# Two-layer GNN kernel: a second rounded copy of layer 0's split rows in two PSUM banks, the product halves in one bank, the last sums of a pair turned behind the next pair's first chunks

## What is computed

```python
agg = jax.ops.segment_sum(x[src], dst, num_segments=N)          # both layers
h = (1.0 + eps) * x + agg                                       # layer 0
h = relu(batch_norm(h @ W1 + b1, g1, be1)); h = relu(batch_norm(h @ W2 + b2, g2, be2))
x = layernorm(x + (x + h))
h = jnp.where(indeg[:, None] > 0, agg, x)                       # layer 1, indeg: edges of a node
h = batch_norm(relu(h @ W.T + b)); x = layernorm(x + h)
```

## Time and profile before

| | us |
|---|---|
| median of 3 runs | 2592.99 (2587.13 to 2593.28) |
| the profiled execution | 2588.04, its span 2586.3 |
| PE busy | 2295.0 (89% of the span) |
| POOL busy | 1602.0 (62%) |
| DVE busy | 1364.4 (53%) |
| ACT busy | 801.0 (31%) |
| granted TensorE clock, mean | 0.950 |

### The profile page before, as it was taken

How to read it: one execution, slowest core, us unless ns; L and a number is a source line. 1 busy time by engine, 2 the same in 40 slices (tenths; PEclk the granted TensorE clock), 3 DMA queues, 4 the chain that set the end, 5 groups by cost and what they waited for, 6 DMA issues and landing times. The chain is left out here.

```text
span 2586.3 us, 41697 instructions
## 1 busy us (share of the span) xinstructions
PE 2295.0 (89%) x9657; PEld 1505.0 (58%) x9658; DVE 1364.4 (53%) x2155; ACT 801.0 (31%) x1272; POOL 1602.0 (62%) x1729
## 2 busy tenths in 40 slices
PE   4999999999999999799995299999999999999964
PEld 2666666666666666688884255555555555555544
DVE  5555555555555555533336555455545555554557
ACT  1333333333333333455548411111111111111157
POOL 6777777777777777100002467777777777777712
PEclk9999999999999999899996699999999999999976
DMA  8777778787877877433216767777777777777758
GB/s 259 233 227 242 224 236 245 220 249 231 242 242 225 251 222 245 142 112 95 93 49 190 255 193 223 210 225 220 219 224 213 226 222 217 223 225 216 224 138 285
DMA packets 180571, 545.11 MB, mean 211 GB/s; under 512 B 48787, under 2 KB 51178, under 8 KB 175794
## 3 DMA queue, kind: packets, MB, share of 16 engines
q0 software_dynamic: 125120, 410.09, 53.5%
q1 hardware_dynamic: 33880, 78.23, 10.1%
q10 hardware_dynamic: 21544, 56.48, 6.5%
HBM read 493.06 MB, written 51.62 MB: 211 GB/s over the span
## 5 line engine op out<-in xcount | busy, mean ns | idle before, releaser
L780 PE MATMUL psum<-ring,select 128*125 x2600 | 1260.9, 608 | 11.0 <-issue 8.7
L555 POOL DMA_INDIRECT ring<-x_in,staged x782 | 799.1, 1022 | 246.2 <-issue 224.0
L555 POOL DMA_INDIRECT ring<-x_d,staged x782 | 748.2, 957 | 261.4 <-issue 226.4
L780 PEld LDWEIGHTS psum<-ring,select 128*125 128x125 f32 x2600 | 479.3, 191 | 380.3 <-issue 336.0
L651 DVE TENSOR_TENSOR rows_lo<-ring,rows_hi 128x512 fp32r<-128x512 f32 x500 | 329.8, 689 | 283.8 <-ACT rows_hi L867 283.2
L867 ACT ACTIVATE rows_hi<-ring 128x512 fp32r x500 | 295.0, 625 | 479.3 <-SPq L523 335.9
L808 PE MATMUL psum<-sumsT_hi,w_hi 128*128 128x250 f32 x1248 | 400.6, 321 | 4.3 <-DVE sumsT_lo L674 4.3
L765 PE MATMUL psum<-rows_hi,select_r 128*125 128x512 f32 x500 | 376.0, 752 | 7.5 <-DVE rows_lo L651 4.2
L808 PE MATMUL psum<-sumsT_lo,w_hi 128*128 128x250 f32 x1248 | 350.1, 281 | 0.0
L808 PE MATMUL psum<-sumsT_hi,w_lo 128*128 128x250 f32 x1248 | 348.4, 279 | 0.0
L808 PEld LDWEIGHTS psum<-sumsT_hi,w_hi 128*128 128x128 f32 x1248 | 237.3, 190 | 36.1 <-issue 32.6
(11 more groups left out here) (168 smaller groups left out, 2255.2 us busy)
## 6 DMA issues: line engine op xcount, KB each, us to landing
hidden_d<-of_layer ACTq DMA_DIRECT2D x25, 1000.0 KB, 5.4
act_f<-hidden_d SPq DMA_DIRECT2D x24, 1000.0 KB
ring<-x_in,staged POOLq DMA_INDIRECT x782, 3.8
ring<-x_d,staged POOLq DMA_INDIRECT x782, 3.7
own<-x_in ACTq DMA_DIRECT2D x50, 224.0 KB
own<-x_d ACTq DMA_DIRECT2D x50, 224.0 KB
ring<-x_d SPq DMA_DIRECT2D x10, 1120.0 KB
x_d<-done_r SPq DMA_DIRECT2D x9, 1120.0 KB
```

The source lines that it names most:

```text
L555: nc.gpsimd.indirect_dma_start(slot(s), None, table, bass.IndirectOffsetOnAxis(ap=staged[:, s:s + 1], axis=0)).then_inc(gathered[s], 16)
L780: whole = nc.tensor.matmul(agg(h), select[h][:, WHOLE_AT.index(p), :], of_chunk(pe, first, place), start=False, stop=n + 1 == WINDOW, skip ...
```

## The change

1. Layer 0: ACT writes each high part twice, to `rows_hi` for PE and to PSUM bank 5 or 7 for DVE, which subtracts from there. So ACT waits, before the pair of writes of k, for DVE to be done with k - 2.
2. Layer 0: bank 5 is freed by putting all products of the loop in bank 4 (one bank in place of two). The very last ones use banks 4 and 0.
3. Both layers: PE clears bank 0, starts the pair's first two chunks, and only then waits for the second tile's sums, clears bank 1 and turns (`between` in `scatter`).
4. Layer 1: the edge counts are taken out of `selection` and stand later in DVE's order (`counts`).

```diff
+        high_ps = [m.bank(5), m.bank(7)]
+        AHEAD = 2 if layer == 0 else 0
+        PRODUCT_BANKS = 1 if layer == 0 else 2
+        def prod_ps(b, last):
+            return m.bank(4 if b % 2 == 0 or layer == 0 and not last else 0 if layer == 0 else 5)
...
@@ low_rows
-                        nc.vector.tensor_tensor(rows_lo[:, k, :], of_chunk(dve, first, SPLIT_AT[k]),
-                                                rows_hi[:, k, :].bitcast(F32), ALU.subtract).then_inc(split_lo, 1)
+                        high = high_ps[k % 2] if layer == 0 else rows_hi[:, k, :].bitcast(F32)
+                        nc.vector.tensor_tensor(rows_lo[:, k, :], of_chunk(dve, first, SPLIT_AT[k]), high, ALU.subtract
+                                                ).then_inc(split_lo, 1)
@@ DVE's loop
                         low_part(v)
+                        if layer == 1:
+                            counts(v, 0)
...
                         low_rows(v, 1, first[1], 0, 4)
+                        if layer == 1:
+                            counts(v, 1)
@@ scatter
                     for n, p in enumerate(ORDER):
+                        if n == 2:
+                            between()
@@ turn
                     for h in range(2):
                         pe.wait_ge(sums_done[h], job + 1)
+                    if bank is not None:
+                        at = within(pe, bank * m.BANK, 2 * m.BANK, "bank 1 or 2")
+                        clear(m.psum[0:z.NT, bass.ds(at, 1)])
@@ PE's loop
-                    clear(i, 0)
-                    clear(i, 1)
+                    pe.wait_ge(sums_done[0], i * groups + 1)
+                    clear(agg(0)[:, 0:1])
+                    pe.reg_mov(cleared, 1)
                     with pe.Fori(0, groups) as g:
                         v = of_use(pe, i, groups, g)
-                        turn(v)
-                        scatter(i, v, g, tiles(i, 0), 0)
-                        scatter(i, v, g, tiles(i, 1), 1)
+                        scatter(i, v, g, tiles(i, 0), 0, lambda: turn(v, pe.snap(cleared, min_val=1, max_val=2)))
+                        scatter(i, v, g, tiles(i, 1), 1, lambda: None)
+                        pe.reg_mov(cleared, 2)
@@ high_rows
                         act.wait_ge(split_used, SPLIT * (2 * v + h) + k + 1)
+                        if layer == 0:
+                            act.wait_ge(split_lo, SPLIT * (2 * v + h) + k + 1)
                         act.wait_ge(landed, i * per_pair + first + (SPLIT_AT[k] + 1))
-                        nc.scalar.activation(rows_hi[:, k, :], of_chunk(act, first, SPLIT_AT[k]), ACT.Copy
-                                             ).then_inc(split_hi, 1)
+                        high = nc.scalar.activation(rows_hi[:, k, :], of_chunk(act, first, SPLIT_AT[k]), ACT.Copy)
+                        if layer == 0:
+                            high = nc.scalar.activation(high_ps[k % 2].bitcast(F32R), of_chunk(act, first, SPLIT_AT[k]),
+                                                        ACT.Copy)
+                        high.then_inc(split_hi, 1)
```

More of the change, by code:

```diff
@@ L602, in _ @@
                 if layer == 0:
+                    nc.vector.sem_inc(split_lo, AHEAD)
+                if layer == 0:
                     setup.vector(dve)
@@ L638, in selection, with counts @@
                                             ).then_inc(select_done[h], 1)
[L639 to L646, removed]
+                def counts(v, h):
+                    dve.wait_ge(select_done[h], 2 * v + 2)
+                    with nc.allow_low_precision(reason="counts up to WINDOW are exact in bfloat16"):
+                        nc.vector.tensor_reduce(edge_count[h][:, 0, :],
+                                                select_r[h][:].bitcast(F32).rearrange("p k n -> p n k"), AX.X, ALU.add)
+                        nc.vector.tensor_reduce(edge_count[h][:, 1, :], select[h][:].rearrange("p k n -> p n k"),
+                                                AX.X, ALU.add).then_inc(counted[h], 1)
                 def low_rows(v, h, first, a, b):
@@ L747, in agg, with clear, scatter @@
                     return m.bank(h)[0:z.NT, :]
[L749 to L754, removed]
+                def clear(out):
+                    nc.tensor.matmul(out, m.zeros[:, 0:z.NT], m.ones[:, 0:1], start=True, stop=False,
+                                     skip_group_check=True)
+                def scatter(i, v, g, tile, h, between):
                     tile_use = pe.snap(2 * v + h)
@@ L785, in scatter, with turn @@
                             product(v, PRODUCT_AT[h][n + 1])
-                def turn(job):
+                def turn(job, bank=None):
                     pe.wait_ge(lo_done, 2 * job + 1)
@@ L796, in turn, with product @@
                     last.then_inc(turned, 1)
-                def product(job, b):
+                def product(job, b, final=False):
                     if b == 0:
@@ L801, in product @@
                         pe.wait_ge(weights_lo, W_PARTS)
-                    pe.wait_ge(product_out, HALVES * job + b + 1)
+                    pe.wait_ge(product_out, HALVES * job + b + (1 if layer == 1 or b == 0 or not final else 0))
                     for o in (2 * b, 2 * b + 1):
-                        out = prod_ps[:, b % 2, (o % 2) * z.W:(o % 2 + 1) * z.W]
+                        out = prod_ps(b, final)[:, (o % 2) * z.W:(o % 2 + 1) * z.W]
                         parts = [(w, s, k) for k in range(z.KD)
@@ L832, in _ @@
                 for b in range(HALVES):
-                    product(uses, b)
+                    product(uses, b, final=True)
             @block.scalar
             def _(act):
-                nc.scalar.sem_inc(product_out, 2)
+                nc.scalar.sem_inc(product_out, PRODUCT_BANKS)
                 if layer == 0:
@@ L875, in read_product @@
                     for o in (2 * b, 2 * b + 1):
-                        from_ = prod_ps[:, b % 2, (o % 2) * z.W:(o % 2 + 1) * z.W]
+                        from_ = prod_ps(b, last)[:, (o % 2) * z.W:(o % 2 + 1) * z.W]
                         if layer == 0:
@@ L884, in read_product @@
                     nc.scalar.sem_inc(product_out, 1)
-                    if layer == 0 and b == HALVES - 1 and store:
+                    if layer == 0 and b == HALVES - 1 and not last:
                         act.dma_start(m.hidden_d[bass.ds(pair * P, P), :], hidden.rearrange("p k n -> p (k n)")
@@ L929, in _ @@
                 for b in range(HALVES):
-                    read_product(uses, z.PAIRS - 1, b, store=False)
+                    read_product(uses, z.PAIRS - 1, b, last=True)
 def batch_norm_constants(nc, z, m, dve_sem, act_sem, dve, act, gamma, beta, scale, bias, blocks, tmp):
```

9 lines of the change are left out of this document (6 added, 3 removed).

## The result

| | before | after |
|---|---|---|
| median, us | 2593.14 (2587.13 to 2593.32, 4 runs) | 2562.97 (2558.62 to 2565.32, 4 runs) |
| the profiled execution | 2588.04 | 2563.73, its span 2562.0 |
| mean granted TensorE clock | 0.950 | 0.964 |

The forecast was 12.5 us.

What follows compares the result with a forecast made beforehand. Two limits within 3%, PE's sequence and POOL's gathers, were taken to bound both layers; afterwards PE sets layer 0. Layer 0 -1.5 and layer 1 -11 us made 2593 - 12.5 = 2580.5 us, range 2545 to 2606.

Steps and rivals of the forecast that it cites:

- the second copy at 0.50: Layer 0, ACT: each extra write of a high part to PSUM was taken to cost 0.50 us, bounds 0 to 0.53.
- k0: Layer 0, first split row of a pair's first tile: PE ready at 3.0, row at 4.4, stall 1.4 us.
- k6: Layer 0, split row behind product 0: ready 3.8 us after the product's end, PE wants it at 3.5, 0.3 late.
- From the first of these activations to k2 pass 2.64 us.: Layer 0, ACT: split row k2 starts 2.64 us after the turned sums' first activation, stalling PE 1.75 us.
- E + 10.6: Layer 0, E being PE's end of a pair's last chunk: product 0 starts 10.6 us after it, 1.05 us late.
- rival 1: Layer 0 becomes bound by the gathers, if k0 and k2 come 1.2 us sooner: 2524 to 2551 us; 15%.
- the start point was 40.40: Layer 0 before: mean 40.40 us a pair against PE's own 38.97, the 1.4 us lost to the gathers.
- Rival 2: Layer 0 split rows' chain costs more than the turn gives, PE's idle spots risk a low clock: 2611 us; 20%.
- Forecast -11: Layer 1 in all: earlier start, faster gathers and shorter end give -11 us, between -4 and -16.
- The 3 us from the gathers: Layer 1: gathers at 1.25 us set the time after POOL's restart; up to 7 us less, 3 taken.
- the 2 us at the end: Layer 1: last turn follows the last gather after 10.7 us, in layer 0 after 8.8; 2 us gained.
- The single product bank: Product loop: ACT needs 1.4 us to read a product, 4 us lie between products; no cost unless ACT is 3 us late.

## Why the prediction was right in sign and short in size

**Right: what bounds layer 0.** Gathers beside `low_rows` are lengthened by its two SBUF operands, and the read from PSUM takes all of the excess away (1.024 to 0.948 us). The Trainium skill ("SBUF — State Buffer", Who interferes with whom) states the contention, and the traces agree in both layers (layer 1: 0.966 to 0.945). What it says of a probe, in which `tensor_tensor` didn't stall DMAs, doesn't carry over to these gathers: with nothing changed but the place of that operand they take 1.004 and 0.948 us. That PE would then set the pace, POOL waiting for it, was right as well (20.3 us), and so was the second copy at 0.50 (0.58 busy, a distance of 0.52 to 0.54).

**Right: k0, and k6 nearly.** k0's wait was 1.25 us (forecast 1.4), k6 costs 0.1 (0.3).

**The step that failed: "From the first of these activations to k2 pass 2.64 us."** It stacked k2 behind the second copy. But that stretch is not set by ACT's own row of work: it begins when PE has turned, and the own-row loads are issued while the activations still run (the load of 249.45 stands ahead of the activation of 249.95). The extra copies fit in between, k2 starts 3.9 us after the turn's start in both kernels, and the 2.64 us are 1.93 (249.95 to 251.88). Product 0 comes at E + 9.7 in the pair shown instead of the forecast E + 10.6. Over the 23 pairs of the changed kernel from one E to the next the median is E + 9.82; over the 10 pairs of the kernel before that ran at full clock and took at most 39.3 us it was E + 9.45. The term was 1.05 us a pair and is 0.4. Those 10 pairs took 39.06 us at the median; with k6's 0.1 that gives 39.55, and 39.53 was measured, where the forecast had 40.3. 24 x 0.77 = 18.5 us, less 1 us more in the first pair (it lost 2.0 instead of 1): layer 0 gained 19.1 us instead of 1.5. The prediction weighed "k2 1.2 us sooner" as rival 1; k2 came 0.8 us sooner, and the result lies between the forecast and that rival. That the sum came within 18 us of the median is in part luck: layer 0 was forecast 17.6 us too slow and layer 1 8.4 us too fast.

**What was missing: why the start point was 40.40.** The prediction put it to the gathers alone and used the low clock only as a risk. The runs show two limits of equal pace: with the gathers freed and the turn early, low clocks hold a pair at 40.87 us; with the turn late and the gathers not freed (and no copy), the gathers hold it at 40.37; freed gathers and a full clock together give 39.53, or 39.60 with the early turn filled. Rival 2 had it that new idle spots of PE would lower the clock. Between the second and the last turn of layer 0 there was no low clock left at all. The waits for k0 and k2 stand apart, between matmuls, and the wait and the turn no longer stand in one piece; that this is the reason is argued, not shown.

**Layer 1: the sign right, the size too large.** Forecast -11, and -2.6 in the profile. The start was nearly right: the 21st gather came 4 us sooner (32.7 to 28.8; forecast 5 to 6). With the early turn it came as soon (28.8), so that this is the late counts' doing. The 3 us from the gathers did not come, and of the 2 us at the end 0.7. The mean gather went from 0.957 to 0.966 us: as many as before overlap a subtraction, which here still reads two SBUF operands (91 and 90), but 34 instead of 21 take longer than 1.1 us. With the early turn, filled or not, the mean was 0.955 to 0.957. The profiled execution of the changed kernel is the longest of four that hold the same code in layer 1 (1006.8, and 1001.5, 1000.4, 1003.0 in the kernels with the copy unread, without the copy, and with the own rows later): their mean is -6.5 us. Why the late turn lengthens more gathers is not settled.

**The single product bank** cost nothing on the chips of the first kind, as forecast: no trace there has PE waiting for ACT's read. On the slower chips it did: in every kernel with one bank PE waits 37 to 52 us for it in layer 0. The prediction had said that this would show if ACT were late by 3 us. It wasn't tried apart.

**Left open.** Why the unread copy still has gathers of 1004 ns against 1023 without it: the subtractions are then spaced further apart, and the longest gather takes 1.46 instead of 2.00 us, but the cause is only argued. The late counts alone were not measured on a chip of the first kind. What makes ACT's reads of the products late on three of the chips was not found.

## What to carry to other kernels

When two limits lie within a few per cent of each other (here gathers at 41.5 us a pair and PE with a falling clock at 40.9), undoing the parts of a change one at a time can show little for each, since only the pair pays; make the experiment that lifts both before a part is called useless. Count a stretch from the event that releases it on the other engine, not from the instruction that happens to stand first in it: then the trace of before already shows whether new work fits in. And put transfers that nobody waits for soon, here the own-row loads, behind the work that the critical engine waits for: that one move brought 22 us (2563.0 to 2540.4), three quarters of what the whole change did.

## What the runs showed of the hardware

- With a wait of 1.3 to 1.8 us followed by eight transposes, at the same place of every pair, PE's granted clock fell in 23 of 24 pairs of one kernel; in the kernel before, with waits of 1.0 to 3.3 us there, in 11 of 24. The clock stayed full when 1.36 us of small matmuls on zeros stood ahead of that wait (2596.7 to 2562.4 us, by 20 instructions a pair that compute nothing).
- GpSimd's indirect gathers took 1.004 us on average where DVE's subtraction read both operands from SBUF, and 0.948 where one came from PSUM.
- A DMA can be issued from ACT's queue while activations that stand ahead of it are still to finish: the load was issued at 249.45 us, 0.5 us before the activation at 249.95.
- Chips differ by 20% for the same kernel (2591 to 3124 us), with gathers that take POOL as long. The second copy with its read from PSUM and the single product bank are together worth 0.6% on one kind (2578 to 2563 us); unread, they cost 1.4% on the other (3036 to 3079).
